# Attention output transposed on TensorE through ps_m instead of by a transposing DMA, in a fused attention and feed-forward block

## The reference

```python
xn = _layernorm(x)                                  # x: 8 x 2048 x 1024
# attention, 16 heads of 64
att = q @ k.T / sqrt(64) / temperature + slope_h * (k_pos - q_pos), causal
y   = softmax(att) @ v                              # 2048 x 1024
att_out = y @ W_proj + b_proj
# feed-forward on the same normalised input, int weights scaled by 1/127
h = silu(xn @ wg.T) * (xn @ wu.T)                   # 2048 x 3072
return x + att_out + h @ wd.T
```

## Time and profile before

| | |
|---|---|
| three runs, median (lowest to highest) | 1151.06 us (1150.41 to 1236.3) |
| the profiled execution's own time | 1151.06 us |
| its span, slowest core (core 1) | 1149.5 us |
| spans of the eight cores | 1144.0 to 1149.5 us |
| TensorE busy on core 1 | 1101.4 us (96%) |
| VectorE, ScalarE, GpSimd busy | 585.8, 516.1, 266.6 us |

### The profile page before, as it was taken

The page is one execution under the profiler, slowest core; times in us unless marked ns, Lnnn a source line. Parts: engine busy times, 40 slices in busy tenths (PEclk is TensorE's granted clock), DMA queues, the critical chain, the costliest instruction groups (busy, mean ns, idle before and its releaser), DMA issues.

```text
span 1149.5 us, 24412 instructions; the slowest of 8 cores (1144.0 to 1149.5 us)
## 1 busy us (share of the span) xinstructions
PE 1101.4 (96%) x7702; PEld 562.9 (49%) x7702; DVE 585.8 (51%) x1190; ACT 516.1 (45%) x933; POOL 266.6 (23%) x289
## 2 busy tenths in 40 slices
PE   3899899999999999999999999999999999999998
PEld 1344455555555555555555555555555344444443
DVE  5441766666666676676666666666773100000110
ACT  1443456655655665565565566556666200000000
POOL 6210121222221222132222112112223432222220
PEclk9999999999999999999999999999999999999999
DMA  8439033433413432153321313113521652525222
GB/s 181 134 89 178 20 61 70 75 75 66 88 35 66 80 79 65 39 89 70 65 57 29 66 43 62 34 31 69 170 61 33 220 188 74 183 74 183 74 74 74
DMA packets 57055, 98.37 MB, mean 86 GB/s; under 512 B 23284, under 2 KB 43893, under 8 KB 55846
## 3 DMA queue, kind: packets, MB, share of 16 engines
q0 software_dynamic: 7872, 35.66, 16.5%
q1 hardware_dynamic: 46178, 52.65, 15.7%
q10 hardware_dynamic: 2884, 8.50, 1.9%
HBM read 90.49 MB, written 27.26 MB: 102 GB/s over the span
## 4 chain that ended last, share of the span: by engine, by line
PE 88%; DVE 5%; issue 3%; DMA 2%; ACT 1%; POOL 1%; DVEq 0%; ACTq 0%; POOLq 0%; SPq 0%
PE ps_gu L724 25%; PE ps_dn L885 14%; PE ps_s L815 10%; PE ps_t L796 10%; PE ps_m L704 9%; PE ps_y L831 5%; PE ps_dn L880 5%; PE ps_t L764 5%; DVE cm L553 2%; DMA xstage<-xin 2%; PE ps_m L844 1%; PE ps_s L818 1%; PE ps_t L800 1%; DVE st L501 1%; DVE hst L489 1%
## 5 line engine op out<-in xcount | busy, mean ns | idle before, releaser
L553 DVE TENSOR_REDUCE cm<-ps_s 128x1 f32<-128x512 f32 (+3 forms) x640 | 379.9, 608 | 195.0 <-PE ps_s L815 112.0
L660 ACT ACTIVATE pt<-ps_t 128x512 bf16<-128x512 f32 (+1 forms) x576 | 327.2, 575 | 241.6 <-PE ps_t L796 151.3
L724 PE MATMUL ps_gu<-xnT,wubuf 128*128 128x512 bf16 x768 | 262.0, 378 | 2.3 <-DVE hst L489 2.3
L724 PE MATMUL ps_gu<-xnT,wgbuf 128*128 128x512 bf16 x768 | 261.3, 378 | 1.2 <-ACT kst L605 1.2
L815 PE MATMUL ps_s<-kx,qx 67*128 67x512 bf16 (+3 forms) x640 | 213.5, 347 | 9.7 <-DVE cm L553 8.2
L796 PE MATMUL ps_t<-qx,kx 98*128 98x512 bf16 (+3 forms) x640 | 216.4, 348 | 2.0 <-ACT pt L660 1.8
L431 POOL TENSOR_SCALAR th_s<-th_s 128x512 f32<-128x512 f32 x96 | 59.1, 616 | 621.4 <-ACT th_s L613 621.4
L885 PE MATMUL ps_dn<-wdres,hb 128*128 128x512 bf16 x768 | 168.5, 379 | 0.0
L831 PEld LDWEIGHTS ps_y<-Vt,pt 128*128 128x128 bf16 x2176 | 125.3, 97 | 81.9
L831 PE MATMUL ps_y<-Vt,pt 128*128 128x65 bf16 x2176 | 138.8, 193 | 0.0
L594 DVE SCALAR_TENSOR_TENSOR outsb<-ps_dn,xres 128x512 f32<-128x512 f32 x32 | 20.7, 686 | 205.1 <-PE ps_dn L885 205.1
(11 more groups left out here) (74 smaller groups left out, 753.8 us busy)
## 6 DMA issues: line engine op xcount, KB each, us to landing
h_sc<-hst SPq DMA_DIRECT2D x96, 128.0 KB, 1.8
hb<-h_sc SPq DMA_DIRECT2D x4, 3072.0 KB, 14.0
xstage<-xin SPq DMA_DIRECT2D x16, 512.0 KB, 6.1
xres<-xin POOLq DMA_DIRECT2D x16, 512.0 KB, 4.8
out<-outsb ACTq DMA_DIRECT2D x15, 512.0 KB, 2.7
wgbuf<-wg_r POOLq DMA_DIRECT2D x12, 512.0 KB, 6.3
wubuf<-wu_r POOLq DMA_DIRECT2D x12, 512.0 KB, 8.9
wd_sc<-wd_r POOLq DMA_DIRECT2D x12, 512.0 KB, 8.1
```

What stands on the lines that cost most here:

```text
L553: e.tensor_reduce(cm[:, c0:c0 + 1], ps_s[:, s % 2 * 512:s % 2 * 512 + w], AX.X, AluOpType.max, negate=True).then_inc(sem["v_mx"], 1)
L660: e.activation(pt[t % NPT][:, 0:w], ps_t[:, t % 2 * 512:t % 2 * 512 + w], AF.Exp).then_inc(sem["a_e"], 1)
L724: mm = e.matmul(ps_gu[:, r // 8 * 512:r // 8 * 512 + 512], w[:, w0:w0 + 128], xnT[:, dc * T + tb * 512:dc * T + tb * 512 + 512], start=(dc ...
```

## The change

The `yt` entry becomes work for TensorE and ScalarE. TensorE waits for `v_y`, multiplies the four 128 x 128 parts of `ysb[b]` with the identity into `ps_m` and signals `p_yt`. ScalarE copies `ps_m` (128 x 512) into `YT` and signals `a_yt`. SyncE issues nothing for it any more. The entry joins the list `m_users`, and the planner now sets `misc_free = k + 2` behind it. The waits for the transposing DMAs are replaced: VectorE's before it overwrites `ysb[b]` and SyncE's before the load into `hb0` by waits for `p_yt`, TensorE's ahead of the bias matmuls by one for `a_yt`.

```diff
@@ attention_plan
                 M = ("yt", n, 0)
                 n_yt += 1
+                misc_free = k + 2
@@ m_users
-            elif M[0] == "qk" and M[2]:
+            elif M[0] == "yt":
+                n_yt += 1
+                m_users.append(("a_yt", n_yt))
+            elif M[2]:
@@ sync
-                if M is not None and M[0] == "yt":
-
-                    n = M[1]
-                    p, b = n // 8, n % 4
-                    e.wait_ge(sem["v_y"], n + 1)
-                    y0 = p * T + b * 512
-                    e.dma_start_transpose(out=YT[:, y0:y0 + 512].rearrange("p (i q) -> p i q", i=4),
-                                          in_=ysb[b][:, :]).then_inc(sem[f"l_yt{b}"], 16)
...
-                    for b in range(4):
-                        e.wait_ge(sem[f"l_yt{b}"], 16 * NHP)
+                    e.wait_ge(sem["p_yt"], 4 * NHP)
@@ vector
-                        e.wait_ge(sem[f"l_yt{b}"], 16 * p)
+                        e.wait_ge(sem["p_yt"], 4 * (p - 1) + b + 1)
@@ scalar
+                elif M[0] == "yt":
+                    n = M[1]
+                    p, b = n // 8, n % 4
+                    n_yt += 1
+                    e.wait_ge(sem["p_yt"], n_yt)
+                    e.activation(YT[:, p * T + b * 512:p * T + (b + 1) * 512], ps_m[:, :], AF.Copy).then_inc(
+                        sem["a_yt"], 1)
@@ tensor
-                if M is None or M[0] == "yt":
+                if M is None:
                     continue
...
+                elif M[0] == "yt":
+                    n = M[1]
+                    e.wait_ge(sem["v_y"], n + 1)
+                    for i in range(4):
+                        mm = e.matmul(ps_m[:, i * 128:(i + 1) * 128], ysb[n % 4][:, i * 128:(i + 1) * 128],
+                                      ident_s[:, :], start=(i == 0), stop=(i == 3))
+                    mm.then_inc(sem["p_yt"], 1)
+                    n_m += 1
...
-            for b in range(4):
-                e.wait_ge(sem[f"l_yt{b}"], 16 * NHP)
+            e.wait_ge(sem["a_yt"], 4 * NHP)
```

More of the change, by code:

```diff
@@ L39 @@
     "l_gu0", "l_gu1", "s_wd", "l_wd", "l_wp", "s_h0", "s_h1", "s_h2", "s_h3",
[1 row of a table removed]
[1 row of a table added]
     "g_set", "g_th", "g_s", "g_xr",
     "v_t", "v_cbq", "v_ln", "v_xn", "v_q", "v_mx", "v_mc", "v_rc", "v_y", "v_h", "v_out",
-    "a_c", "a_sd", "a_xe", "a_v", "a_k", "a_m", "a_e", "a_th", "a_g", "a_b",
-    "p_c", "p_xT", "p_v", "p_qk", "p_s", "p_m", "p_t", "p_av", "p_g", "p_u", "p_b", "p_d", "p_dl",
+    "a_c", "a_sd", "a_xe", "a_v", "a_k", "a_m", "a_e", "a_yt", "a_th", "a_g", "a_b",
+    "p_c", "p_xT", "p_v", "p_qk", "p_s", "p_m", "p_t", "p_av", "p_yt", "p_g", "p_u", "p_b", "p_d", "p_dl",
 )
@@ L285, in m_free @@
             return m_users[n]
-        n_q, n_k = 4, 4
+        n_q, n_k, n_yt = 4, 4, 0
         for _, _, _, M in steps:
@@ L651, in _ @@
             evac_k(0, NTB - 1)
+            n_yt = 0
             for k, (_, t, _, M) in enumerate(steps):
@@ L671, in _ @@
                                  AF.Copy).then_inc(sem["a_m"], 1)
-                elif M[0] == "qk" and M[2] and M[1] % 2:
+                elif M[0] == "yt":
[5 more added lines that the diff above has]
+                        sem["a_yt"], 1)
+                elif M[2] and M[1] % 2:
                     evac_k(M[1] // 8 + 1, M[1] % 8 // 2)
```

## The result

The changed kernel takes 1156.78 us (median of four runs, 1156.03 to 1157.23). The kernel before took 1150.74 us in the same comparison. The ratio is 1.0056 with a 95% interval of 1.0041 to 1.0070: 6.4 us slower, by the interval 4.7 to 8.1.

A forecast was written before the change was run, and what follows sets the result against it. TensorE, busy 1101.4 of 1149.5 us, was taken to bound the kernel. Matmuls 6.8 plus copy 0.4 less pauses 0.3 gave 6.9 us on 1151.06: 1158.0 us, range 1152 to 1167.

The forecast's parts named there:

- The bound: In the attention stretch TensorE is busy 685.05 of 694 us, so work added to it is paid in full outside pauses.
- Four matmuls, 0.22 us: At each of 32 `yt` entries, four 128 x 128 matmuls cost TensorE 0.22 us; 31 entries count, 6.8 us.
- The wait for `v_y`: TensorE's wait for `ysb` before the new matmuls costs 0, since VectorE is ready 1.85 us ahead, 0.74 at the last.
- The last entry's 0.22 us: At the loop's end the matmuls push a gate tile by 0.22 us, absorbed by TensorE's 0.51 us wait for `hst`.
- ScalarE's copy, 0.4 us: 32 copies from `ps_m` into `YT` delay exponentials that TensorE needs: 0.4 us, ends 0 and 18.9.
- `ps_m` one step longer: The bank's next user waits for `a_yt`; the planner leaves two steps, and later `qk` entries add no work: cost 0.
- The pauses that shorten, -0.3 us: Some TensorE pauses for VectorE's maxima end earlier as VectorE gains 0.22 us per entry: 0.3 us back, ends 0 and 6.8.
- The DMA gives nothing back: Removing the 32 transposing DMAs from SyncE's queue saves nothing, as TensorE waits on none of them.
- The sum of 6.9 us: Over the whole kernel, 6.8 for matmuls plus 0.4 for copies less 0.3 for pauses, giving 1158.0 us, 0.6% more.
- the pauses: Rival, chance 0.07: TensorE's pauses behind the new matmuls shrink by as much, so not slower, 1151 us.
- the copy: Rival, chance 0.06: ScalarE's copies hold exponentials past the scores that need them, 14.4 us on top, about 1172 us.
- the 1201 us: Rival, chance 0.01: each 128 x 128 transposition on TensorE costs the page's 390 ns, adding 49.9 us.

The follow-up runs named there:

- the doubling: The changed kernel with each transposition's four matmuls done twice, 256 new matmuls instead of 128: 1164.78 us, ratio 1.0117 to the kernel before.
- the plan alone: The kernel before with only the planner's line `misc_free = k + 2` behind a `yt` entry, no instruction added: ratio 0.9991.

## Why the prediction was right

*The bound.* TensorE's busy time grew by 6.4 us between the two pages, by 6.7 in the loop of core 1, and the loop by 6.8. That work on the full engine is paid for in full was the decisive reading, and the doubling shows it best: 6.8 us for the first set, 6.7 for the second.

*Four matmuls, 0.22 us.* Right to the last digit that the profile has: 0.22 at 197.92, and 0.21 to 0.22 from the loops. The row of the same shape was the one to take, not L844's 0.24.

*The wait for `v_y`.* 0 as predicted: no idle time stands before the new matmuls.

*The last entry's 0.22 us.* Wrong by its whole size. The pause shrank as predicted, from 0.51 us to 0.29. But the prediction followed only the tile whose result had been late already, not the gate tile that was pushed. Its tanh came 0.22 us later, and so did its `hst`. Timeline of PE at the end of the loop on core 1, before:

```profile
892.55 1.89 PE L724 MATMUL ps_gu<-xnT,wgbuf 128*128 128x512 bf16 x8
894.34 1.89 PE L724 MATMUL ps_gu<-xnT,wubuf 128*128 128x512 bf16 x8
```

and in the changed kernel:

```profile
892.01 0.39 PE L855 MATMUL ps_m<-ident_s,ysb 128*128 128x128 bf16 x4
892.24 1.89 PE L727 MATMUL ps_gu<-xnT,wgbuf 128*128 128x512 bf16 x8
894.42 1.89 PE L727 MATMUL ps_gu<-xnT,wubuf 128*128 128x512 bf16 x8 [0.29 <-DVE hst L484]
896.14 1.89 PE L727 MATMUL ps_gu<-xnT,wgbuf 128*128 128x512 bf16 x8
898.16 1.89 PE L727 MATMUL ps_gu<-xnT,wubuf 128*128 128x512 bf16 x8
```

From one up tile to the next it was 894.34 - 890.83 = 3.51 us, and is now 898.16 - 894.42 = 3.74. The pause had no slack behind it: `hst` and TensorE met at 894.34. The tile behind these starts at its old distance from the last product with V again (11.8 us), the next one is late again, and so on by turns. The last up tile is one of the late ones, and hands its delay on to the bias matmuls, before and now:

```profile
917.62 1.89 PE L724 MATMUL ps_gu<-xnT,wubuf 128*128 128x512 bf16 x8 [0.25 <-DVE hst L489]
```

```profile
921.45 1.89 PE L727 MATMUL ps_gu<-xnT,wubuf 128*128 128x512 bf16 x8 [0.50 <-DVE hst L484]
```

That is 30.9 and 31.15 us behind the last products with V at 886.7 and 890.3. With both the matmuls and the copy moved behind tile 88's way the 3.51 us are back. It is the step "they are absorbed", and it measures 0.25 us. It is no fixed price of a pushed gate tile, though. The run with the matmuls and the DMA pushes that tile as well, and its stretch is 41.9 us: `hst` comes later still in it, up to the last up tile but one, and the last one doesn't wait for it at all. What else holds `hst` in these places wasn't settled.

*ScalarE's copy, 0.4 us.* 0.1 us net of the DMA's removal, inside its bounds, and the waits on the exponential fell rather than rose. The doubled copy shows how near the limit was: 4.0 us.

*`ps_m` one step longer.* 0 was right for the bank, on which nothing waits. That a `qk` entry a step later costs nothing was wrong by 0.2 us, as the plan alone showed.

*The pauses that shorten, -0.3 us.* The three waits sum to 9.8 us instead of 10.2, so the size was right on core 1, but not by the reason given. The waits for `hst`, which the prediction placed only partly behind the loop, lie wholly behind it, so their fall gives the loop nothing. The wait for the maxima rose by 0.9 us, about half of that by the plan, and the other two fell. Net the loop shows nothing of it.

*The DMA gives nothing back.* Right for the loop (771.0 us without it, 770.9 with it). Of the whole kernel's 1.7 us the profile places 0.3; the rest stays open.

The sum of 6.9 us met 6.8 + 0.25 in the profile and 6.4 in the runs. The mechanism was right, and that the sum came so near is partly luck: the matmuls in the loop cost 6.5 us instead of 6.8, and two terms that the prediction had at nothing cost 0.2 (the plan) and 0.25 (the last entry). The prediction also took 2% for what a measurement of this kernel can tell; the interval is 0.15% to either side, so a change of 0.56% is clear of noise.

Of the rivals, the pauses fell by the doubling, the copy by its own absence, the 1201 us from the Trainium skill's figure by 128 matmuls that cost 55 ns each. "VectorE: DVE Perf Modes" of the Trainium skill, in "The three transpose paths", gives the DMA crossbar 1309 ns for the 128 x 128 case; here such a DMA (`mt`, 128 x 128) landed 2.2 to 11.9 us after its issue, beside the loop's other transfers, and how late the two hops landed decided how many of the maxima could go by DMA.

## What to carry to other kernels

Ask of a transposition which engine is full and how long the reader can wait. In this kernel TensorE is 96% busy. Where the reader is at least nine steps (12 us) away, the DMA cost next to nothing, while each group of four matmuls costs its distance, 0.22 us. Where the reader is fewer steps away, the large transfers issued around the DMA decide, on its own queue and perhaps on another engine's, and a wait of some us eats dozens of saved matmuls. Before calling a delay absorbed by a pause, follow what the delayed work itself feeds one tile further.

## What was not expected of the hardware

The transposing DMAs of the maxima landed after 2.2 to 2.3 us as a median, those of `ysb` after 2.4 to 2.5 us in the kernel before, where the latest took 8.3 to 11.1 us depending on the core. One behind eight loads of 512 KB in the same queue took 11.9 us.

Waits of TensorE cost more than their own length. Where it stood for 487 us in 44 waits, the loop of that core was 556 us longer, although 64 groups of matmuls had gone from it, and the granted clock of the stretch was 0.80 of the 2.4 GHz level. After the single wait of 6.1 us with 45 units by DMA it was 0.80 for 13 us, having been 1.00 from 780 to 800 us.
